# Attention orders annealed anew and 128-row blocks moved forward in a fused attention and expert kernel

## The reference

```python
x = x + attention(layernorm(x), Wq, Wk, Wv)        # x: 8 x 512 x 256, one causal head of 256
x = x + ffn(layernorm(x))
# ffn: shared expert + two routed experts for each of the 4096 rows
shared = (silu(x @ shared_gate.T) * (x @ shared_up.T)) @ shared_down.T       # I = 512
probs  = sigmoid(x @ router_w.T + routing_bias)                              # 8 experts
scores, indices = top_k(probs, 2); scores = scores / sum(scores)
routed = sum over the two of score * ((silu(x @ gate_w[e]) * (x @ up_w[e])) @ down_w[e])
```

## Time and profile before

| | us |
|---|---|
| median of 3 runs | 573.29 (572.55 to 575.23) |
| the profiled execution, its own time | 578.4 |
| its span, first to last instruction | 576.6 |
| TensorE busy | 521.9 (91%) |
| VectorE busy | 371.8 (64%) |
| ScalarE busy | 306.5 (53%) |
| GpSimd busy | 290.2 (50%) |

### The profile page before, as it was taken

How to read it: one execution, slowest core, us unless ns; L and a number is a source line. 1 busy time by engine, 2 the same in 40 slices (tenths; PEclk the granted TensorE clock), 3 DMA queues, 4 the chain that set the end, 5 groups by cost and what they waited for, 6 DMA issues and landing times. The chain is left out here.

```text
span 576.6 us, 14723 instructions
## 1 busy us (share of the span) xinstructions
PE 521.9 (91%) x4521; PEld 422.9 (73%) x4522; DVE 371.8 (64%) x933; ACT 306.5 (53%) x578; POOL 290.2 (50%) x236
## 2 busy tenths in 40 slices
PE   2797999798999999889799999999999999999970
PEld 1455788586777878778578888888888888888860
DVE  5579999879897978969645555455545455545440
ACT  4989778577768667544234443443444443444430
POOL 3654778557585846756014434533433343533443
PEclk9699999899999999989999999999999999999996
DMA  7988866929493948552455646565565555566523
GB/s 260 221 202 149 155 171 132 257 78 217 140 198 125 199 134 170 175 156 76 91 115 88 99 76 94 75 93 74 74 96 81 78 77 75 83 90 77 73 30 36
DMA packets 147551, 70.53 MB, mean 122 GB/s; under 512 B 122384, under 2 KB 140560, under 8 KB 147504
## 3 DMA queue, kind: packets, MB, share of 16 engines
q1 hardware_dynamic: 133904, 50.69, 42.1%
q0 software_dynamic: 13600, 19.22, 19.0%
HBM read 19.48 MB, written 23.54 MB: 75 GB/s over the span
## 5 line engine op out<-in xcount | busy, mean ns | idle before, releaser
L1767 PE MATMUL bank<-xn2t,w 128*128 128x256 f16 x1728 | 197.1, 273 | 2.9 <-DMA xn2t<-rows 2.5
L1767 PEld LDWEIGHTS bank<-xn2t,w 128*128 (+1 forms) x1728 | 168.5, 98 | 26.5 <-issue 2.8
L712 POOL DMA_INDIRECT out<-p,wm x56 | 89.2, 1593 | 115.2 <-DMA out<-p,wm 44.6
L1336 DVE SCALAR_TENSOR_TENSOR th<-th,bank 128x512 f32<-128x512 f32 x88 | 60.1, 683 | 75.3 <-ACT th L806 75.2
L1781 PE MATMUL bank<-w,h 128*128 (+1 forms) x840 | 98.5, 273 | 2.1 <-DVE z L1268 2.0
L1781 PEld LDWEIGHTS bank<-w,h 128*128 128x128 f16 x840 | 81.5, 98 | 13.5 <-DVE z L1268 3.5
L762 ACT ACTIVATE h<-th 128x512 f16<-128x512 f32 x72 | 45.2, 628 | 85.3 <-DVE th L1345 83.5
L806 ACT ACTIVATE th<-bank 128x512 f32<-128x512 f32 x88 | 52.5, 596 | 58.4 <-PE bank L1767 58.2
L1171 DVE TENSOR_TENSOR h<-th,h 128x512 f16<-128x512 f32 x72 | 49.8, 691 | 41.1 <-ACT h L762 41.1
L601 POOL TENSOR_TENSOR w<-wst,w 128x768 f16<-128x768 f32 x36 | 59.1, 1642 | 31.4 <-ACT w L762 31.1
L625 POOL DMA_INDIRECT rows<-xrow,sidx x56 | 57.4, 1026 | 27.5 <-DVE sidx L1328 15.9
(11 more groups left out here) (159 smaller groups left out, 728.3 us busy)
## 6 DMA issues: line engine op xcount, KB each, us to landing
wst<-w_all SPq DMA_DIRECT2D x36, 384.0 KB, 3.6
x<-x SPq DMA_DIRECT2D x8, 512.0 KB, 5.6
out<-x SPq DMA_DIRECT2D x8, 512.0 KB, 4.6
rows<-xrow POOLq DMA_DIRECT2D x1, 1192.5 KB, 7.3
rows<-xrow,sidx POOLq DMA_INDIRECT x56, 4.3
out<-p,wm POOLq DMA_INDIRECT x56, 4.0
wm<-rows SPq DMA_DIRECT2D x28, 9.0 KB, 1.8
xn2t<-rows SPq DMA_TRANSPOSE x28, 3.6
```

What stands on the lines that cost most here:

```text
L712: cc.indirect_dma_start(out, bass.IndirectOffsetOnAxis(ap=index, axis=0), part, None, compute_op=ALU.add).then_inc(y_out, 16)
L1336: d.scalar_tensor_tensor(out=tb, in0=tb, scalar=1.0, in1=G[half][:, :], op0=ALU.add, op1=ALU.mult).then_inc(f_sg, 1)
L1767: ins = mm(dst, w_ap(j, ws, m * MAT + k * I + (2 * half + i) * P, P), moving(ms * KD + k), start=(cnt == 0), stop=(cnt == 3 * KD - 1))
```

## The change

Every engine's order of the attention part is new: the prologue, the body of `iteration(i)`, and the last iteration (i = 7), which now stands written out by itself with an order of its own, so that `iteration(i)` runs for 3 to 6. Nothing in the lists is added or left out; the helpers are the same calls in another order.

In the routed part the entry loads are split: `load_pair` becomes `load_pair_rows` and `load_pair_aux`, and rows go before aux; at the entry the four row transposes go first, then the four aux loads. The first two groups hold the gate-ups of singles 0 to 4 and the downs of 0 to 3. From group 2 on, gate-up is of single i+3 and down and add are of i+2. Group 12 has no single gate-up, group 13 no single at all. On SP, `hs_transpose(i+2)` is now the first call of group i and not the second, and the loads of the single stand before those of the first pair. `single_down(0)` and `single_down(1)` come one call later in the first group. At the end the adds are pair 25, pair 26, pair 27.

The diff, cut to the iteration bodies and to what the steps below speak of (SP first, then GpSimd, VectorE, TensorE). ScalarE's list is reordered in the same way: in the last iteration `tanh(12, 0)`, `xn2_normalise(7, 0)`, `xn2_high(7, 0)`, `tanh(12, 1)`, `split_h(12, 0)`, `xn2_normalise(7, 1)`, `xn2_high(7, 1)`; and at the end `w_high(34)`, `w_high(35)`, `split_h(15, 1)`.

```diff
+            w_load(0)
+            w_load(1)
             x_load(2)
             x_load(3)
-            w_load(0)
-            w_load(1)
...
             def iteration(i):
 
                 w_load(4 * i + 1)
+                w_load(4 * i + 2)
                 xn2_transpose(i - 1, 0)
-                w_load(4 * i + 2)
+                xn2_transpose(i - 1, 1)
                 p_transpose(i, 0)
-                xn2_transpose(i - 1, 1)
+                xn_transpose(i + 1)
                 p_transpose(i, 1)
                 p_transpose(i, 2)
-                xn_transpose(i + 1)
+                p_transpose(i, 3)
                 w_load(4 * i + 3)
-                p_transpose(i, 3)
+                w_load(4 * i + 4)
                 out_base(i - 3)
                 x_load(i + 3)
-                w_load(4 * i + 4)
-
-            for i in range(FILL, B):
+
+            for i in range(FILL, B - 1):
                 iteration(i)
+            w_load(29)
+            xn2_transpose(6, 0)
+            p_transpose(7, 0)
+            xn2_transpose(6, 1)
+            p_transpose(7, 1)
+            w_load(30)
+            p_transpose(7, 2)
+            p_transpose(7, 3)
+            w_load(31)
+            w_load(32)
+            xn2_transpose(7, 0)
+            w_load(33)
+            xn2_transpose(7, 1)
+            out_base(4)
             out_base(5)
-            w_load(33)
             w_load(34)
-            xn2_transpose(7, 0)
-            xn2_transpose(7, 1)
             w_load(35)
...
+            def group(i, par, single=True):
+
+                if not isinstance(i, int) or i > 2:
+                    hs_transpose(i + 2, par)
+                if single:
+                    row = single_row(i + 4)
+                    load_single_rows(row, par, i + 3)
+                load_pair(2 * i + 2, 2 - 2 * par, 4 * i + (2 * SHARED + 2), 8 * i + 8 * par, GROUP_ADDS * i)
+                if single:
+                    load_single_aux(row, par, 8 * i + (32 - 8 * par), GROUP_ADDS * i + 48)
+                load_pair(2 * i + 3, 3 - 2 * par, 4 * i + (2 * SHARED + 4), 8 * i + 8 * par, GROUP_ADDS * i + 32)
...
-            load_pair(0, 0, 2 * SHARED - 4, 0, 0)
+            load_pair_rows(pair0, 0, 2 * SHARED - 4)
             sp.wait_ge(tab2, T2_STEPS)
-            load_single(0, 0, 0, 0, 0)
-            load_single(1, 1, 0, 0, 0)
-            load_pair(1, 1, 2 * SHARED - 4, 0, 0)
+            single0, single1 = single_row(0), single_row(1)
+            load_single_rows(single0, 0, 0)
+            load_single_rows(single1, 1, 0)
+            load_pair_rows(pair1, 1, 2 * SHARED - 4)
+            load_pair_aux(pair0, 0, 0, 0)
+            load_single_aux(single0, 0, 0, 0)
+            load_single_aux(single1, 1, 0, 0)
+            load_pair_aux(pair1, 1, 0, 0)
             out_base(6)
             out_base(7)
...
             def iteration(i):
 
+                w_low(4 * i)
+                xn2_low(i - 1, 0)
+                xn2_low(i - 1, 1)
+                scatter(i - 2, 0, 1)
+                rstd1(i + 2)
+                xn_low(i + 1)
+                scatter(i - 2, 1, 3)
+                w_low(4 * i + 1)
                 put_idx(i - 1)
-                scatter(i - 2, 0, 1)
-                xn2_low(i - 1, 0)
-                w_low(4 * i)
-                scatter(i - 2, 1, 2)
-                xn2_low(i - 1, 1)
-                xn_low(i + 1)
-                rstd1(i + 2)
-                scatter(i - 2, 2, 4)
-                w_low(4 * i + 1)
-                scatter(i - 2, 4, 6)
+                scatter(i - 2, 3, 5)
                 w_low(4 * i + 2)
-                scatter(i - 2, 6, 8)
+                scatter(i - 2, 5, 8)
                 w_low(4 * i + 3)
                 rstd2(i)
 
-            for i in range(FILL, B):
+            for i in range(FILL, B - 1):
                 iteration(i)
+            w_low(28)
+            xn2_low(6, 0)
+            scatter(5, 0, 1)
+            xn2_low(6, 1)
+            scatter(5, 1, 2)
+            w_low(29)
+            scatter(5, 2, 8)
+            w_low(30)
+            w_low(31)
+            put_idx(6)
+            rstd2(7)
+            scatter(6, 0, 3)
             table_iota()
             w_low(32)
-            scatter(6, 0, 5)
+            scatter(6, 3, 8)
+            w_low(33)
             put_idx(7)
-            scatter(6, 5, 6)
-            w_low(33)
+            scatter(7, 0, 8)
             w_low(34)
-            scatter(6, 6, 8)
...
-            def group(i, par, first=False):
-
-                if first:
-                    y_add_single(0, 0, 16, 0)
-                else:
-                    y_add(2 * i - 1, 3 - 2 * par, 8 * i + (8 * par), GROUP_ADDS * i - 16)
-                y_add_single(i + 1, 1 - par, 8 * i + (16 + 8 * par), GROUP_ADDS * i + 16)
-                y_add(2 * i, 2 * par, 8 * i + (16 - 8 * par), GROUP_ADDS * i + 32)
...
+            def group(i, par):
+
+                y_add(2 * i - 1, 3 - 2 * par, 8 * i + 8 * par, GROUP_ADDS * i)
+                y_add_single(i + 2, par, 8 * i + (32 - 8 * par), GROUP_ADDS * i + 32)
+                y_add(2 * i, 2 * par, 8 * i + (16 - 8 * par), GROUP_ADDS * i + 48)
+
+            def last_adds():
+
+                i = GROUPS - 1
+                y_add(2 * i - 1, 1, 8 * i + 8, GROUP_ADDS * i)
+                y_add(2 * i, 2, 8 * i + 8, GROUP_ADDS * i + 32)
+                pool.wait_ge(ax_in[3], 8 * GROUPS)
+                pool.wait_ge(y_out, GROUP_ADDS * i + 64)
+                for a in range(2):
+                    pool.wait_ge(y_read, SHARED + PAIRS + a)
...
         @block.scalar
         def _(act):
...
             def iteration(i):
 
-                row_numbers(i - 2)
                 row_max(i, 0)
-                add_shared(2 * i - 5)
+                stats_1(i + 2)
                 row_max(i, 1)
                 minus_max(i, 0)
                 row_max(i, 2)
+                minus_max(i, 1)
+                aggregate_1(i + 2)
+                row_numbers(i - 2)
                 v_low(i, 1)
-                minus_max(i, 1)
-                stats_1(i + 2)
                 p_low(i, 0)
+                add_shared(2 * i - 5)
                 minus_max(i, 2)
-                aggregate_1(i + 2)
                 ffn_gate(2 * i - 4, 0)
+                p_low(i, 1)
+                ffn_up(2 * i - 4, 0)
                 row_max(i, 3)
-                ffn_up(2 * i - 4, 0)
-                p_low(i, 1)
+                p_low(i, 2)
                 minus_max(i, 3)
-                p_low(i, 2)
                 ffn_gate(2 * i - 4, 1)
+                ffn_low(2 * i - 4, 0)
                 ffn_up(2 * i - 4, 1)
-                ffn_low(2 * i - 4, 0)
+                shift_1(i + 2)
+                row_sums(i)
+                ffn_gate(2 * i - 3, 0)
+                ffn_low(2 * i - 4, 1)
+                read_logits(i - 1)
+                ffn_up(2 * i - 3, 0)
                 p_low(i, 3)
-                shift_1(i + 2)
-                ffn_low(2 * i - 4, 1)
-                ffn_gate(2 * i - 3, 0)
-                row_sums(i)
-                ffn_up(2 * i - 3, 0)
-                read_logits(i - 1)
+                route(i - 1)
                 ffn_gate(2 * i - 3, 1)
-                route(i - 1)
+                add_shared(2 * i - 4)
+                ffn_up(2 * i - 3, 1)
+                weights(i - 1)
                 add_attention(i, 0, 1)
-                ffn_up(2 * i - 3, 1)
-                add_shared(2 * i - 4)
                 ffn_low(2 * i - 3, 0)
...
+            row_max(7, 0)
+            minus_max(7, 0)
+            add_shared(9)
+            row_max(7, 1)
+            row_numbers(5)
+            minus_max(7, 1)
+            row_max(7, 2)
...
             ffn_gate(14, 0)
             weights(7)
-            add_shared(12)
-            places(7)
-            ffn_low(13, 1)
-            row_numbers(7)
             ffn_up(14, 0)
             ffn_gate(14, 1)
+            places(7)
+            row_numbers(7)
+            ffn_low(14, 0)
+            table_of_pairs()
             ffn_up(14, 1)
-            ffn_low(14, 0)
+            ffn_gate(15, 0)
             add_shared(13)
-            table_of_pairs()
             ffn_low(14, 1)
-            ffn_gate(15, 0)
             ffn_up(15, 0)
+            table_of_singles()
+            ffn_low(15, 0)
+            add_shared(14)
             ffn_gate(15, 1)
             ffn_up(15, 1)
-            ffn_low(15, 0)
-            add_shared(14)
             ffn_low(15, 1)
-            table_of_singles()
 
             def single_h(k):
 
...
             def iteration(i):
 
@@ -1993,35 +2149,50 @@
                 scores(i, 3, 4)
                 shared_gate_up(2 * i - 4, 1)
                 shared_gate_up(2 * i - 3, 0)
+                logits(i - 1)
                 shared_gate_up(2 * i - 3, 1)
-                logits(i - 1)
-                pv(i, 0, 2)
                 shared_down(2 * i - 4, 0, 1)
-                pv(i, 2, 3)
+                pv(i, 0, 1)
```

(39 more changed lines are left out.)

529 lines of the change are left out of this document (320 added, 209 removed).

## The result

The changed kernel took **579.01 us** (median of 15 runs, 574.1 to 584.7) against 573.96 for the kernel before in the same comparison (571.86 to 578.34, 15 runs): ratio **1.0064, 95% interval [1.0037, 1.0091]**, slower by 3.7 us where 13.3 less was forecast. (The ratio is the one that the comparison gives, without the run of 584.7, which was in a slower state; the quotient of the two medians would be 1.009, 5.1 us.) Its profiled execution took 575.51 us with a span of 573.8, that is 3.5 under its median, while the profiled one of before lay 4.4 over its own; so this pair of traces shows 2.9 us of gain where the medians show a loss.

What follows compares the result with a forecast made beforehand. TensorE was taken as the bound, busy 521.9 of 576.6 us, with gains only outside the routed groups; terms -0.5 - 5.0 - 2.4 - 1.2 + 0.5 - 4.8 = -13.4 took 573.29 to 559.9, say 560, range 554.5 to 568.

Steps and rivals of the forecast that it cites:

- First routed groups: Start of the routed part: row transposes before entry loads and a later single_down(0) cover TensorE's row waits, -1.2 us.
- Steady groups: Routed groups: TensorE gains nothing; the later h transpose fits by 0.2 us at its median, +0.5 us, bounds 0 and +12.
- The rival built on it: Steady groups: single_down waits for the h transpose in each of 11 groups, at 1.6 us each 577 us; chance 0.04.
- Tail: Behind the last matmul: the new order of adds shortens the late chain from 6.0 to 1.2 us, -4.8 us.
- Attention iterations: To 211.8 us: four P waits, a clock dip and three z waits go, less new small waits, -5.0 us.
- the feared new waits for xn2: Attention iterations: logits come earlier than the second xn2 transpose, some 0.6 us in each of four iterations, +2.4 us.
- The lock as a loss: Rival: one or two GpSimd w_low block a short operation of table_of_singles, +1.6 to +3.3 us, 561.6 to 563.3; chance 0.08.
- Last iteration and entry: Iteration 7 to first routed rows: logits(7) 1.6 us earlier and 0.8 off the chain behind them, -2.4 us.
- Opening: Kernel start: earlier w loads 0 and 1 shorten the 8.0 us wait for wm, -0.5 us, bounds -2 and +1.
- a gap at the entry: Sign of a wrong forecast: over 2.5 us between the last shared down and the first routed gate-up.

Runs made afterwards that it cites:

- x3: The change with the h transpose of single i+3 issued a group ahead, behind the group's first pair load: 575.6 us, ratio 0.9991 to the kernel before.
- x1: The change unaltered, run again for a second trace: 580.4 us, ratio 1.0072 to the kernel before.
- x9: The kernel before, unchanged, traced on the third chip: 586.3 us, ratio 1.0006.
- x11: Only the change's attention orders, routed part as before, on the third chip: 583.3 us, ratio 0.9968 to the kernel before.
- x5: Only the change's attention orders, routed part as before, on the second chip: 584.9 us, ratio 0.9993 to the kernel before.
- x6: Only the change's routed part, attention part as before, on the second chip: 595.6 us, ratio 1.0184 to the kernel before.
- x13: The change with entry loads of singles 2 and 3 behind row loads and h transposes a group earlier: 583.4 us, ratio 0.9981 to the kernel before.
- x14: x13's kernel with the eighth attention iteration and work up to the routed part in the old order: 581.2 us, ratio 0.9945 to the kernel before.
- x15: x13's kernel with row 5's run of six scatters split two by two between low-half passes on GpSimd: 578.2 us, ratio 0.9907 to the kernel before.
- x7: x4's kernel with the zeroing of the row table (and the put_idx after it) back in its old place: 584.7 us, ratio 0.9995 to the kernel before.
- x8: x7's kernel with w load 30 put behind the last two P transposes on SP: 583.6 us, ratio 0.9981 to the kernel before.
- x17: x15's kernel with row 7's eight scatters also split three, three and two between low-half passes: 582.9 us, ratio 1.0052 to the kernel before.
- x12: x4's kernel on the third chip: 583.1 us, ratio 0.9961 to the kernel before.
- x4: The change with entry loads of singles 2 and 3 behind row loads and h transposes a group earlier: 569.5 us, ratio 0.9900 to the kernel before.
- x16: x15's kernel again, on the fifth chip: 571.7 us, ratio 0.9842 to the kernel before.
- x18: Only the change's attention orders, with the last iteration's scatters apart as in x15: 572.4 us, ratio 0.9866 to the kernel before.
- x2: The change with the entry loads of singles 2 and 3 behind the row loads of single 3 and pair 3: 575.6 us, ratio 0.9998 to the kernel before.

## Why the prediction was wrong

**First routed groups** is the step that failed. It read "the row transposes all go before the 9 KB and 4.5 KB loads", and took 1.2 us off. That holds for the eight loads of the entry alone (pairs and singles 0 and 1). In the first group behind them the entry load of single 2 stands between pair 2 and the rows of single 3. I never walked SP's queue through it. Its threshold had gone from 16 to 48 too, since the pair's adds now come first on GpSimd; the full diff shows it. Cost: +9.7 in place of -1.2; taking it away gave 4.8 us alone and, with the next step mended, 6.1 (575.6 to 569.5).

**Steady groups** was right in mechanism and too small. The forecast had the h transpose land with 0.2 us to spare and took +0.5, bounds 0 and +12. The waits are there, 0.7 us in two for h and 3.0 in seven "issue" gaps at the single gate-up that follows: 4.1 us of idle in 215, and x3 removes all but 0.07. Why the lateness shows as a gap behind single_down more than as a wait before it is not shown. The rival built on it (577, chance 0.04) named the right place; its price of 1.6 us a group did not come, 0.4 did. That its 577 lies near the measured 579 is chance: most of the loss came from the entry.

**Tail**: -4.8 forecast, -5.2 in the profiled pair, -3.1 in x1. In the profiled pair the last pair's adds start 0.7 us behind the last matmul (forecast 1.2), and they wait for their data now, not for the chain:

```profile
564.64 1.55 POOL L764 DMA_INDIRECT out<-p,wm  x1 [2.90 <-ACT p L1253]
```

In x1 they start 2.7 us behind it and do wait for the chain of adds. The tail of before varies as well: 15.1 us in its first trace, 12.5 in x9, where x10, the change on the same chip, has 11.7. So the mechanism is there, and its size agrees with the forecast partly by luck of the pair.

**Attention iterations**: forecast -5.0. In the profiled pair -9.5, x1 against before -5.7, x11 against x9 -7.0. P(3) in front of `xn_transpose` and the logits ahead of shared_down did what was said; of the feared new waits for xn2 one came, of 0.8 us at logits(2). Something that I had not seen, and whose worth no run here takes by itself: most small vector operations no longer fall on a GpSimd low-half pass. Of `row_sums` the mean is now 241 ns:

```profile
L1520 DVE TENSOR_SCALAR s<-sums 128x4 f32<-128x4 f32 x8 | 1.9, 241 | 0.0
```

against a mean of 1281 before (median 1546). This is the other side of the rule of the Trainium skill, SBUF — State Buffer, section "Who interferes with whom", that the prediction had only as a loss: the order decides who is locked out, and here it moved the short ones out of the way. The trace agrees with the rule. The lock as a loss fell on another place than the rival's: the write of the routing weights into `xrow` took 1.41 us beside a low-half pass (its median is 0.19), in the chain to `cumh`, for which TensorE then waited 2.3. The lock is 1.2 of it; the rest is that `counts` now follows `prefix(7)` directly on TensorE.

```profile
246.01 1.41 DVE L1409 SCALAR_TENSOR_TENSOR xrow<-wv_,rden 128x32 f32<-128x32 f32 x1
...
245.71 1.65 POOL L646 TENSOR_TENSOR w<-wst,w 128x768 f16<-128x768 f32 x1
```

**Last iteration and entry**: forecast -2.4, measured -2.7 (x1 -2.1), with one new wait for P of 2.0 at logits(6), where w load 30 stands ahead of the last two P transposes, and 2.3 for `cumh`. On three of five chips it was a loss instead: 7.7 (x11 against x9), 8.8 (x5 against x6) and 7.9 us (x13 against x14). The trace of the kernel before, on its one chip, shows nothing of the kind. The new run of six scatters ahead of `w_low(30)` was plain in the diff, but my sum has no term for moved scatters; breaking up that run and the next took back 5.6 of the 7.9 on one chip (x15).

**Opening**: -0.5 forecast, +0.6 at logits(0), and the first t_product 1.7 later. It waits for the transposed xn (9.7 us) and no more for `wm`. The prediction had that transpose issued as before; in fact the zeroing of the row table had moved to the start, and with it back the product starts at 18.5 and 17.8 (x7, x8).

The sum of the parts as x1 shows them (+1.4 - 5.7 - 2.1 + 11.2 - 3.1 = +1.7 against the profiled span of 576.6 us) has the sign of the result. The range of 554.5 to 568 left out the case that decided. The sign listed under "wrong", a gap at the entry, was looked for before the first routed gate-up and stood 29 us behind it.

## What to carry to other kernels

When loads are reordered, walk each queue through the first and last groups by themselves: a load that waits for a slot stops every transfer behind it, and a peeled group need not have the loop's order. A transfer that just fits by the median of its landing can be late in some of its instances, so move it a group ahead while there is room, as x3 does. Time an order on more than one chip. Where chips like those of x5 to x15 have to be served, don't issue long runs of indirect scatters beside work whose signals another engine waits for; one experiment (x15) speaks for it, and x17 shows that a scatter put behind a pass that waits costs more.

## What the runs showed of the hardware

**Late signals.** On three of five chips (x5 to x15) a finished matmul's signal reached a waiting engine up to 5 us late (that of logits(6) in x12, 224.2 to 229.3) while GpSimd issued a run of indirect scatters, and came about 1 us behind the last of them. TensorE's own matmuls were held up in the same stretches, with gaps of 0.97 and 1.04 us between them in x9. On the other two chips (x1 to x4, x16 to x18) no such wait or gap stands in any trace, x4's and x15's kernels included. Breaking up two runs removed one wait and shortened another (x13 to x15). What holds TensorE and its signals up, and why only on some chips, is not shown. The kernel before is slower on these three chips too (584.4 to 585.5 us against 577.1 and 579.2).

**The clock.** In x4 TensorE waited 3.05 us for P at logits(6); the nine matmuls behind the wait took 1.16 us and the next twelve 1.47, and the granted clock from 208 to 240 was 1.00. In x2, on the same chip and with the same order up to there, it waited 3.13 and the nine took 1.92, the next twelve 2.42. In x12, on another chip, a wait of 2.25 was followed by nine in 2.10. So the price of a wait of 2 to 3 us is not fixed, even on one chip.
